# An attention and quantised-linear kernel: regrouped opening tiles, a reordered DMA queue in seven units, and q loads issued by ScalarE

## The chip, the cores and the metric

The kernel runs on one core of a Trainium2 chip. The metric is the device time of one execution in microseconds (us). Three runs of the kernel before gave 1568.5, 1568.98 and 1569.91 us, so the median is 1568.98.

## What is computed

```python
x  = L0_attn_x                              # 8 x 1024 x 256, f32
xn = layernorm(x)
q  = xn @ Wq.T   # 16 heads of 16;   k, v = xn @ Wk.T, xn @ Wv.T   # 8 kv heads, each used by 2 heads
energy = q @ k.T - |i - j| * 2 ** -(head + 1)
attn   = softmax(energy / 4) @ v
ffn    = int8(round(xn / x_scale)) @ weight_q.T * x_scale * weight_scale + bias   # x_scale = max|xn| / 127 per token
out    = x + (attn @ Wo.T + bo) + ffn
```

## The kernel before, in words

There are 64 tiles of 128 tokens (`TILES`) and 64 **units**, one for each pair of batch element and kv head (`UNITS`, `KV_HEADS` = 8, two query heads each). Every engine runs a program of its own, written out by hand; semaphores join them.

**Tiles.** A tile is normalised, turned, multiplied by the weights of q and k, and q and k are split into three bf16 parts. The parts are stored to `parts_dram`; tokens' scales go by `token_dram`. The first 11 tiles (`PREP_AHEAD`) are made before any unit, in one loop on each of PE, ScalarE (`find_high`, `keep_xn_t`, `find_middle`), VectorE (`normalise`, `first_stats`, `find_first_largest`, `find_rest`) and GpSimd (`find_rstd`, `find_low`). Tiles 2 and 3 of each four use the buffer `parts_more`: `wait_stored` holds tile 7 until tile 3 is stored. Later tiles are made two at a time in odd units, at block c = 1.

**Sets.** A unit needs a set: rows of k and of q for two heads, copied by DMA from `parts_dram` into one of four slots (`k_set`, `q_set`). `load_set` issues 11 loads (5 of k, 3 of q for each head) and, from set 3 on, two more with the rows of the position bias. Sets 0 to 2 are loaded at the start: set 0 needs tiles 0 to 7. `load_again` copies part of a set to other partitions, after waiting for the whole set. `place_max(u)` puts the negated row maxima of unit u into the set, in four small DMAs. `store_att` and `load_att_t` carry the attention output. All of these DMAs are issued by SP, in program order: a wait in one of them holds every later one.

**Units.** In unit u PE computes, in 8 blocks (c), four score halves (`col_half`), the row scores of later units (`ahead_row_block`: head 1 of unit u+1 in blocks 0 to 3, head 0 of unit u+2 in blocks 4 to 7), and `pv_block`. ScalarE exponentiates each half, GpSimd multiplies the diagonal block (`weigh_near`), VectorE reduces the row scores (`reduce_block`, 16 per unit). PE can begin unit u only when its set is whole, with the four DMAs of `place_max(u)`. `place_max(u + 1)` waits for `turn_max(u + 1)`, which VectorE runs in block 5 of unit u.

**Late sets.** Sets 8, 16, ..., 56 (`late_set`) need tiles that are only just stored. They are loaded at the very end of the unit three before, and unit u = 6, 14, ..., 54 has to run `load_again(u + 2)` early, on a load that is still in flight. SP's order in such a unit is: next x, x turned, `load_again(u + 2)`, set u+3, the token load, `place_max(u + 1)`, `store_att(u - 1)`, `load_att_t`, `load_again(u + 3)`.

**Opening rows.** Before unit 0, PE runs 24 row blocks (`first_row_block`: units 0 and 1), each read by one reduction, with other work between them (`first_others`, placed by `OTHERS_BEHIND` behind blocks 1, 2, 4, 6, ...): `make_v(t)` waits until ScalarE has kept the previous v (`keep_v`).

Of the kernel before, what the change touches and what calls it, by code (L numbers as in the profile page):

```python
# [35 lines left out]
P = 128  # L36
# [153 lines left out]
def build(nc, x, x_t, wqk_t, wv_t, wo_t, wo_last_t, w8_t, w_scale, bias_attn, bias_lin, q_alibi, k_alibi, diag,  # L190
          eye, parts_dram, token_dram, att_dram, out):
    ctx = ExitStack()
    with ctx:
# [232 lines left out]

        block = ctx.enter_context(nc.Block())
# [3 lines left out]
        def _(sp):  # L431
# [20 lines left out]
            def load_set(u, slot):  # L452

                g, tok = u % KV_HEADS, (u // KV_HEADS) * SEQ

                def rows(dst, chunk, row, pick, loaded=set_loaded[slot]):
                    for at, q_parts, k_parts in PAIRS:
                        use = q_parts if pick == "q" else k_parts
                        n = len(use)
                        cols = bass.ds(chunk * TOKENS + tok, SEQ)  # L460
                        here = dst[at:at + n * HEAD_DIM, :]
                        if len(set(use)) == 1:
                            src = parts_dram[bass.ds(row, HEAD_DIM), use[0]:use[0] + 1, cols]
                            sp.dma_start(here, src.rearrange("d j n -> j d n").broadcast_to(  # L464
                                [n, HEAD_DIM, SEQ])).then_inc(loaded, 16)
                        elif list(use) == sorted(use):
                            src = parts_dram[bass.ds(row, HEAD_DIM), use[0]:use[0] + n, cols]
                            sp.dma_start(here, src.rearrange("d j n -> j d n")).then_inc(loaded, 16)  # L468
                        else:
                            for j, part in enumerate(use):  # L470
                                src = parts_dram[bass.ds(row, HEAD_DIM), part:part + 1, cols]
                                sp.dma_start(here[j * HEAD_DIM:(j + 1) * HEAD_DIM, :],  # L472
                                             src.rearrange("d j n -> (d j) n")).then_inc(loaded, 16)

                pairs = KV_HEADS // (QK_CHUNKS - 1)
                rows(k_set[:, slot, :], QK_CHUNKS - 1, g * HEAD_DIM, "k",
                     first_rows_loaded if u == 0 else set_loaded[slot])
                for e in range(GROUP):
                    rows(q_set[:, slot, e, :], g // pairs, (g % pairs * GROUP + e) * HEAD_DIM, "q",
                         first_rows_loaded if u == 0 and e == 0 else set_loaded[slot])  # L480
                if u >= SETS - 1:
                    load_alibi(u, slot)
# [118 lines left out]
            def unit(u, f):  # L601
# [18 lines left out]
                if f["token"]:  # L620
                    load_token(u + 1 + PREP_AHEAD)
                if not f["last"]:
                    place_max(u + 1, (u + 1) % SETS)
                if f["prev"] and u % PAIR == 0:
                    store_att(u - 1)
                for t in f["next_att"]:
                    load_att_t(t, t % 2)
# [39 lines left out]
        def _(pool):  # L667
# [182 lines left out]
            def unit(u, f):  # L850
                t = u + PREP_AHEAD
                for c in range(BLOCKS):
# [12 lines left out]
                    if c == 3:  # L865
                        for made in f["made"][1:]:
                            split_middle(made)
                    if c == 4:
# [621 lines left out]
```

## Time and profile before

| | |
|---|---|
| median of three runs | 1568.98 us |
| the profiled execution, whole time | 1568.38 us |
| its span in the trace | 1566.4 us |
| PE busy | 1497.0 us, 96% |
| VectorE busy | 1394.6 us, 89% |
| ScalarE busy | 1184.8 us, 76% |
| GpSimd busy | 1076.1 us, 69% |
| chain that ended last | PE 47%, VectorE 30%, SP's queue 9%, issue 8%, DMA 3% |

Time is counted from the start of the span. A unit's start, wherever it is given, is the start of the first exponential of that unit on ScalarE. PE is TensorE, DVE VectorE, ACT ScalarE, POOL GpSimd, SP the engine that issues DMAs; SPq is time in which it issues one. PEclk is the granted clock of TensorE, 1.00 being full speed. "L464" is line 464 of the kernel.

### The profile page before, as it was taken

The page shows a single profiled execution, that of the slowest core. Times are in us where ns is not written, and L with a number is a line of the kernel's source. Part 1 is how long each engine was busy: PE and PEld are TensorE (multiplying, and loading weights), DVE is VectorE, ACT ScalarE, POOL GpSimd, SP SyncE. Part 2 cuts the span into 40 slices and gives each one's busy share as a digit, 9 for nine tenths or more (in the row PEclk, how much of TensorE's full clock was granted, in tenths as well). Part 3 has the DMA queues.
Part 4 walks back from the last instruction along what each step waited for, and adds up shares of the span by engine and source line. Part 5 has one row for each costly group of instructions (what it writes and reads, how often), then busy time and mean ns, then how long its engine had stood idle before and what let it go on. Part 6 is the DMA issues. An engine that isn't in the chain of part 4 may idle for free.

```text
span 1566.4 us, 42517 instructions
## 1 busy us (share of the span) xinstructions
PE 1497.0 (96%) x16284; PEld 583.0 (37%) x16284; DVE 1394.6 (89%) x1698; ACT 1184.8 (76%) x2331; POOL 1076.1 (69%) x1627
## 2 busy tenths in 40 slices
PE   5899999999999999999989999999999999999998
PEld 5333333333333333333333334333333333333333
DVE  5999989999899998999979999899998988999981
ACT  3467777777787776887767887777877777788885
POOL 5467777777788876787757877677877776533332
PEclk9999999999999999999999999999999999999999
DMA  6522243333334334333333433433333332312212
GB/s 169 140 76 71 74 100 81 93 98 81 105 83 108 96 79 109 91 92 101 84 92 94 105 85 91 103 98 96 97 83 96 94 92 65 82 49 68 72 44 62
DMA packets 197291, 140.98 MB, mean 90 GB/s; under 512 B 107040, under 2 KB 165728, under 8 KB 197088
## 3 DMA queue, kind: packets, MB, share of 16 engines
q1 hardware_dynamic: 197088, 138.27, 34.2%
q8 instruction: 129, 2.11, 0.6%
q14 instruction: 74, 0.61, 0.1%
HBM read 81.40 MB, written 35.63 MB: 75 GB/s over the span
## 4 chain that ended last, share of the span: by engine, by line
PE 47%; DVE 30%; SPq 9%; issue 8%; DMA 3%; POOL 2%; ACT 0%; POOLq 0%; DVEq 0%; ACTq 0%
DVE row_max L999 27%; PE ps_ring L1279 15%; PE ps_pv L1355 13%; PE ps_row L1296 9%; PE ps_ring L1395 4%; PE ps_ring L1415 3%; SPq L464 2%; SPq L468 2%; SPq L506 2%; DMA q<-neg_max_t 1%; SPq L472 1%; PE ps_ring L1398 1%; DMA k<-k_alibi 1%; DVE pv_turned L1039 1%; PE ps_ring L1409 1%
## 5 line engine op out<-in xcount | busy, mean ns | idle before, releaser
L999 DVE TENSOR_REDUCE row_max<-ps_row 128x1 f32<-128x1024 f32 x1024 | 1199.5, 1213 | 114.7 <-PE ps_row L1298 99.4
L1171 ACT ACTIVATE probs<-ps_ring 128x512 f32<-128x512 f32 x2048 | 1084.5, 601 | 245.2 <-PE ps_ring L1279 242.6
L1279 PE MATMUL ps_ring<-q,k 122*32 122x512 bf16 x8192 | 636.6, 383 | 19.9 <-DMA q<-neg_max_t 19.0
L762 POOL TENSOR_TENSOR probs<-probs,near 128x256 f32<-128x256 f32 x512 | 375.2, 733 | 324.8 <-ACT probs L1171 318.9
L1355 PE MATMUL ps_pv<-probs,v_unit 128*32 128x512 f32 x4096 | 533.5, 596 | 0.0
L1279 PEld LDWEIGHTS ps_ring<-q,k 122*32 122x32 bf16 x8192 | 215.1, 95 | 518.0 <-ACT probs L1171 324.7
L1296 PE MATMUL ps_row<-k,q 64*128 64x512 bf16 x944 | 326.2, 385 | 25.8 <-DVE row_max L999 11.4
L1298 PE MATMUL ps_row<-k_again,q_again 64*128 64x512 bf16 x944 | 326.0, 385 | 0.0
L1296 PEld LDWEIGHTS ps_row<-k,q 64*128 64x128 bf16 x944 | 84.2, 93 | 320.3 <-issue 199.6
L1355 PEld LDWEIGHTS ps_pv<-probs,v_unit 128*32 128x32 f32 x4096 | 124.7, 110 | 54.2 <-issue 7.7
L1298 PEld LDWEIGHTS ps_row<-k_again,q_again 64*128 64x128 bf16 x944 | 84.0, 92 | 0.0
L817 POOL CAST parts<-qk 128x384 bf16<-128x384 f32 x53 | 26.7, 504 | 83.2 <-ACT qk L1180 83.2
L1395 PE MATMUL ps_ring<-xn_t,wqk 128*128 128x128 f32 x636 | 79.9, 275 | 0.5 <-ACT probs L1171 0.5
L1395 PEld LDWEIGHTS ps_ring<-xn_t,wqk 128*128 128x128 f32 x636 | 77.0, 192 | 2.5 <-ACT probs L1171 1.3
L1039 DVE STREAM_TRANSPOSE pv_turned<-ps_pv 128x512 f32<-128x512 f32 x64 | 45.2, 707 | 28.4 <-PE ps_pv L1355 28.4
L809 POOL TENSOR_SCALAR xq_t<-xround 128x256 bf16<-128x256 f32 x53 | 57.4, 1082 | 4.5
L801 POOL TENSOR_SCALAR xround<-xt_step 128x256 f32<-128x256 f32 x53 | 57.0, 1076 | 4.5
L689 POOL TENSOR_TENSOR parts<-rest,parts 128x384 bf16<-128x384 f32 x59 | 54.2, 918 | 8.0 <-ACT parts L1127 3.7
L1177 ACT ACTIVATE v_all<-ps_ring 128x128 f32<-128x128 f32 x53 | 14.7, 278 | 58.5 <-PE ps_ring L1398 58.5
L1415 PE MATMUL ps_ring<-wo,att_t 128*128 128x256 f32 x224 | 57.3, 382 | 0.0
L1279 PE MATMUL ps_row<-k,q 120*32 120x512 bf16 x640 | 45.3, 390 | 11.9 <-issue 9.1
L819 POOL TENSOR_TENSOR rest<-qk,parts 128x384 f32<-128x384 f32 x53 | 48.6, 918 | 4.3
(84 smaller groups left out, 1012.0 us busy)
## 6 DMA issues: line engine op xcount, KB each, us to landing
parts_dram<-parts SPq DMA_DIRECT2D x59, 288.0 KB, 3.0
q_again<-q SPq DMA_DIRECT2D x63, 256.0 KB, 3.3
token_b<-token_dram SPq DMA_DIRECT2D x53, 256.0 KB, 4.1
q<-parts_dram SPq DMA_DIRECT2D x128, 96.0 KB
k<-parts_dram SPq DMA_DIRECT2D x256, 32.0 KB
q<-parts_dram SPq DMA_DIRECT2D x128, 64.0 KB
att_dram<-att_unit SPq DMA_DIRECT2D x126, 64.0 KB
att_t<-att_dram SPq DMA_DIRECT2D x56, 128.0 KB, 2.9
```

The lines of the kernel that those rows point to most:

```text
L762: pool.tensor_tensor(here, here, near[:, u % KV_HEADS, :].rearrange("p (e n) -> p e n", e=GROUP), ALU.mult).then_inc(weighted, 1)
L801: pool.tensor_scalar(xround[:, :], xt_step[:, 1, :, :].rearrange("p c n -> p (c n)"), Q_MAX, ROUND, ALU.min, ALU.add).then_inc(xt_rounded, 1)
L809: pool.tensor_scalar(xq_t[:, t % TURNED, :, :].rearrange("p c n -> p (c n)"), xround[:, :], -ROUND, -Q_MAX - 1, ALU.add, ALU.max).then_inc ...
L999: dve.tensor_reduce(row_max[:, par, e, qb:qb + 1], ps_row[qb % 2][:, :], AX_X, ALU.max, negate=True).then_inc(row_max_found, 1)
L1039: dve.transpose(pv_turned[:, :], ps_pv[:, :]).then_inc(pv_read, 1)
L1171: act.activation(probs[:, c % PBUFS, e, h * HALF:(h + 1) * HALF], ring_bank(u, c, e, h), ACT.Exp, scale=SCALE).then_inc(ring_freed, 1)
L1279: mm = pe.matmul(to[at, :], weights[:, at], moving, start=start, stop=stop)
L1296: pe.matmul(ps_row[qb % 2][:, 0:HALF], q_set[0:ROW_K, slot, e, at], k_set[0:ROW_K, slot, 0:HALF], start=True, stop=True)
L1298: pe.matmul(ps_row[qb % 2][:, HALF:SEQ], q_again[ROW_K:2 * ROW_K, u % AGAIN, e, at], k_again[ROW_K:2 * ROW_K, u % AGAIN, :], start=True, s ...
L1355: mm = pe.matmul(ps_pv[32 * j:32 * j + 32, :], v_unit[:, par, c, :], probs[:, c % PBUFS, j // 2, (j % 2) * HALF:(j % 2 + 1) * HALF], start ...
L1395: pe.matmul(bank[:, m * P:(m + 1) * P], wqk[:, c, m * P:(m + 1) * P], xn_t[:, t % TURNED, c, :], start=(c == 0), stop=(c == EC - 1))
L1415: mm = pe.matmul(bank[:, EMBED:2 * EMBED], att_t[:, t % 2, c, :], wo[:, c, :], start=(c == 0), stop=(c == EC - 1))
```

## The change

Six edits:
1. **Opening tiles regrouped.** Tiles 0 to 7 are made first, on every engine. The maxima of those tiles, the statistics of 8 and 9, the scales, and then tiles 8, 9 and 10 follow behind them. Before, all 11 ran in one loop with the maxima inside.
2. **q of sets 0 to 2 by ScalarE.** ScalarE issues these 18 loads behind `find_middle` of tile 10. SP issues the 15 loads of k where it issued both.
3. **SP's order in units 6, 14, ..., 54** (`copied`): token load, `load_again(u + 2)`, `place_max(u + 1)`, `store_att(u - 1)`, `load_att_t`, and only then set u+3. At the end `load_again(u + 3)` as before.
4. **Attention output in even units:** `norm` on GpSimd moves from the end of block 3 into block 4; on VectorE the reciprocal goes from behind row block 5 to behind 7 and `turn_back` from behind 13 to behind 11.
5. **VectorE's tile work in units 0 and 1** is split between block 1 and block 3.
6. **Projections of the last two units** (`project_last`) are issued two at a time (`project_pairs`), and four instead of six come behind the last block.

```diff
@@ load_set on SP
+                load_rows(sp, k_set[:, slot, :], QK_CHUNKS - 1, tok, g * HEAD_DIM, "k", ...)
+                if u >= SETS - 1:
+                    load_q(sp, u, slot)
                 if u >= SETS - 1:
                     load_alibi(u, slot)
@@ unit on SP
-                if u + 2 < UNITS and late_set(u + 2):
+                copied = u + 2 < UNITS and late_set(u + 2)
+                if copied:
+                    if f["token"]:
+                        load_token(u + 1 + PREP_AHEAD)
                     load_again(u + 2, (u + 2) % SETS)
+                    place_max(u + 1, (u + 1) % SETS)
+                    store_att(u - 1)
+                    for t in f["next_att"]:
+                        load_att_t(t, t % 2)
                 if f["row_set"] and not late_set(u + 3):
                     next_set(u + 3)
...
-                if f["token"]:
-                    load_token(u + 1 + PREP_AHEAD)
...
+                if not copied:
+                    if f["token"]:
+                        load_token(u + 1 + PREP_AHEAD)
...
@@ the opening on GpSimd
-            for t in range(PREP_AHEAD):
-                if t + 4 < PREP_AHEAD:
+            for t in range(BLOCKS):
+                if t + 4 < BLOCKS:
                     find_rstd(t + 4, t % 2)
+                find_low(t, t % 2)
+            for t in range(BLOCKS, PREP_AHEAD):
+                find_rstd(t, t % 2)
+            for t in range(BLOCKS, PREP_AHEAD):
                 find_low(t, t % 2)
@@ the opening on VectorE
-            for t in range(PREP_AHEAD):
-                if t + 2 < PREP_AHEAD:
+            for t in range(BLOCKS):
+                if t + 2 < BLOCKS:
                     normalise(t + 2, t % 2)
-                if t + 4 < PREP_AHEAD:
+                if t + 4 < BLOCKS:
                     first_stats(t + 4)
-                if t + 2 < PREP_AHEAD:
-                    find_first_largest(t + 2)
                 find_rest(t, t % 2, early[t % 2][1])
+            for t in range(BLOCKS, BLOCKS + 2):
+                first_stats(t)
+            for t in range(BLOCKS):
+                find_first_largest(t)
+            find_first_scales(0, BLOCKS, 0)
+            for t in range(BLOCKS, BLOCKS + 2):
+                normalise(t, t % 2)
+            first_stats(PREP_AHEAD - 1)
+            find_rest(BLOCKS, 0, early[0][1])
+            normalise(PREP_AHEAD - 1, 0)
+            for t in range(BLOCKS + 1, PREP_AHEAD):
+                find_rest(t, t % 2, early[t % 2][1])
@@ the opening on ScalarE
+            for t in range(BLOCKS, BLOCKS + 2):
+                keep_xn_t(t, early[t % 2][0])
+            for t in range(BLOCKS, PREP_AHEAD):
                 find_high(t, early[t % 2][1])
                 if t + 2 < PREP_AHEAD:
                     keep_xn_t(t + 2, early[t % 2][0])
                 find_middle(t, t % 2)
+            for i in range(FIRST_PARTS):
+                act.wait_ge(first_parts_stored[i], 16 * len(range(i, BLOCKS, FIRST_PARTS)))
+            for u in range(SETS - 1):
+                load_q(act, u, u)
@@ the opening on PE
+            for t in range(BLOCKS, BLOCKS + 2):
+                turn_xn(t, early[t % 2][0])
+            for t in range(BLOCKS, PREP_AHEAD):
                 make_qk(t, early[t % 2][1])
@@ unit on VectorE
-                at_sums, at_norm = (5, BLOCKS) if apart else (3, 3)
+                at_sums, at_norm = (BLOCKS - 1, SLOTS) if apart else (3, 3)
+                made = 1 if u < PAIR else PAIR
...
-                        if i == SLOTS - 3 and apart:
+                        if i == BLOCKS + 3 and apart:
                             turn_back(u - 1)
-                    if c == 1:
-                        for t in f["normed"]:
+                    if c in (1, 3):
+                        for t in f["normed"][here(c)]:
...
@@ the last units on PE
+            def project_pairs(u, c):
+                at = (u - UNITS + 2) * BLOCKS + c - BLOCKS // 2
+                if 0 <= at < BLOCKS and at % 2 == 0:
+                    for i in (at, at + 1):
+                        project_last(0, P, i)
+                if u == UNITS - 1 and c in (BLOCKS - 3, BLOCKS - 1):
+                    for i in (c - BLOCKS + 3, c - BLOCKS + 4):
+                        project_last(1, P - GROUP * HEAD_DIM, i)
```

## Rows read from the trace of the kernel before

**Rows 1.** Waits over the span: who waited for what, us, times, longest.
```profile
PE ps_ring L1279 <- DMA q<-neg_max_t: 19.0, 8, 4.3
```
**Rows 2.** Busy time in stretches, each two whole units: 12-13, 6-7, 14-15, 30-31, 54-55.
```profile
350.49:396.73 46.24, 45.57 (x494) 17.69 (x492) 43.30 (x53) 36.52 (x73) 37.50 (x57) 1.00 0.31 78
208.53:258.00 49.47, 46.30 (x534) 17.17 (x532) 43.19 (x53) 36.09 (x72) 36.28 (x55) 0.97 0.38 96
396.73:446.61 49.88, 46.35 (x542) 18.53 (x540) 43.40 (x53) 36.85 (x74) 37.56 (x57) 1.00 0.40 104
...
775.60:828.17 52.57, 47.81 (x542) 18.71 (x540) 43.40 (x53) 36.93 (x73) 35.56 (x54) 0.97 0.39 102
...
1342.89:1386.84 43.95, 42.43 (x506) 14.54 (x504) 40.34 (x41) 34.93 (x68) 18.33 (x30) 1.00 0.31 82
```
**Rows 3.** Timeline of SP, 396 to 448 us: start, duration, line, transfer, count.
```profile
400.19 0.83 SPq L488 DMA_DIRECT2D k<-k_alibi  x2
...
405.15 0.55 SPq L497 DMA_DIRECT2D k_again<-k  x1
...
424.18 0.71 SPq L468 DMA_DIRECT2D k<-parts_dram  x1
...
430.56 0.83 SPq L488 DMA_DIRECT2D k<-k_alibi  x2
...
434.35 5.61 SPq L440 DMA_DIRECT2D parts_dram<-parts  x2
...
440.77 2.80 SPq L506 DMA_DIRECT2D q<-neg_max_t  x4
```
**Rows 4.** Transfers over the span: KB each, median us from issue to landing.
```profile
token_dram<-token SPq DMA_DIRECT2D x53, 2.0 KB, 4.5
```
**Rows 5.** Timelines of VectorE and of GpSimd, unit 14.
```profile
409.62 0.20 DVE L1017 STREAM_TRANSPOSE neg_max_t<-neg_max 128x32 bf16<-128x32 bf16 x1
...
408.29 0.62 POOL L752 TENSOR_TENSOR att_normed<-pv_turned,rsum 128x256 f32<-128x256 f32 x1
```
**Rows 6.** Timeline of SP, 0 to 80 us.
```profile
29.77 0.72 SPq L468 DMA_DIRECT2D k<-parts_dram  x1
...
32.36 1.10 SPq L464 DMA_DIRECT2D q<-parts_dram  x2
33.51 0.73 SPq L468 DMA_DIRECT2D q<-parts_dram  x1
```
**Rows 7.** Timeline of ScalarE, 0 to 80 us; in brackets the idle time before, and its releaser.
```profile
24.34 0.49 ACT L1121 ACTIVATE probs<-ps_row 128x384 bf16<-128x384 f32 x1 [1.01 <-DMA parts_dram<-probs]
...
30.25 0.52 ACT L1127 ACTIVATE probs<-rest 128x384 bf16<-128x384 f32 x1 [0.62 <-DVE rest L963]
```
**Rows 8.** Timeline of VectorE, 0 to 80 us.
```profile
18.41 0.39 DVE L931 TENSOR_REDUCE amax_first<-probs 128x1 f32<-128x256 f32 x1
...
24.86 0.56 DVE L963 TENSOR_TENSOR rest<-ps_row,probs 128x384 f32<-128x384 f32 x1 [0.75 <-ACT probs L1121]
...
43.97 12.77 DVE L999 TENSOR_REDUCE row_max<-ps_row 128x1 f32<-128x1024 f32 x11 [0.69 <-PE ps_row L1279]
...
60.21 9.17 DVE L999 TENSOR_REDUCE row_max<-ps_row 128x1 f32<-128x1024 f32 x8
```
**Rows 9.** Timeline of PE, 0 to 122 us.
```profile
10.87 2.34 PE L1230 MATMUL ps_row<-probs,wqk 128*128 128x128 f32 x12
...
16.63 1.50 PE L1230 MATMUL ps_row<-probs,wqk 128*128 128x128 f32 x12
...
37.98 1.90 PE L1279 MATMUL ps_row<-k,q 120*32 120x512 bf16 x16 [9.06 <-issue]
...
68.72 0.61 PE L1279 MATMUL ps_ring<-q,k 122*32 122x512 bf16 x8 [0.60 <-DMA q<-neg_max_t]
...
102.89 0.39 PE L1296 MATMUL ps_row<-k,q 64*128 64x512 bf16 x1 [1.91 <-DVE row_max L999]
```
**Rows 10.** Busy time and granted clock in one stretch of the opening.
```profile
33.00:43.00 10.00, 5.02 (x33) 2.60 (x34) 4.75 (x9) 0.28 (x1) 4.34 (x7) 0.51 0.48 120
```

More of the change, by code:

```diff
@@ L425, in wait_stored, with load_rows, load_q @@
                 eng.wait_ge(parts_stored[t % 2], 16 * ((t - PREP_AHEAD) // 2))
+        def load_rows(eng, dst, chunk, tok, row, pick, loaded):
+            for at, q_parts, k_parts in PAIRS:
+                use = q_parts if pick == "q" else k_parts
+                n = len(use)
+                cols = bass.ds(chunk * TOKENS + tok, SEQ)
+                here = dst[at:at + n * HEAD_DIM, :]
+                if len(set(use)) == 1:
+                    src = parts_dram[bass.ds(row, HEAD_DIM), use[0]:use[0] + 1, cols]
+                    eng.dma_start(here, src.rearrange("d j n -> j d n").broadcast_to(
+                        [n, HEAD_DIM, SEQ])).then_inc(loaded, 16)
+                elif list(use) == sorted(use):
+                    src = parts_dram[bass.ds(row, HEAD_DIM), use[0]:use[0] + n, cols]
+                    eng.dma_start(here, src.rearrange("d j n -> j d n")).then_inc(loaded, 16)
+                else:
+                    for j, part in enumerate(use):
+                        src = parts_dram[bass.ds(row, HEAD_DIM), part:part + 1, cols]
+                        eng.dma_start(here[j * HEAD_DIM:(j + 1) * HEAD_DIM, :],
+                                      src.rearrange("d j n -> (d j) n")).then_inc(loaded, 16)
+        def load_q(eng, u, slot):
+            g, tok, pairs = u % KV_HEADS, (u // KV_HEADS) * SEQ, KV_HEADS // (QK_CHUNKS - 1)
+            for e in range(GROUP):
+                load_rows(eng, q_set[:, slot, e, :], g // pairs, tok, (g % pairs * GROUP + e) * HEAD_DIM, "q",
+                          first_rows_loaded if u == 0 and e == 0 else set_loaded[slot])
         block = ctx.enter_context(nc.Block())
@@ L454, in load_set @@
                 g, tok = u % KV_HEADS, (u // KV_HEADS) * SEQ
[L456 to L480, printed above, removed]
+                load_rows(sp, k_set[:, slot, :], QK_CHUNKS - 1, tok, g * HEAD_DIM, "k",
+                          first_rows_loaded if u == 0 else set_loaded[slot])
+                if u >= SETS - 1:
+                    load_q(sp, u, slot)
                 if u >= SETS - 1:
@@ L619, in unit @@
                     load_att_last(1, P - GROUP * HEAD_DIM, UNITS - 1)
-                if f["token"]:
-                    load_token(u + 1 + PREP_AHEAD)
[L622 to L627, printed above, removed]
+                if not copied:
+                    if f["token"]:
+                        load_token(u + 1 + PREP_AHEAD)
+                    if not f["last"]:
+                        place_max(u + 1, (u + 1) % SETS)
+                    if f["prev"] and u % PAIR == 0:
+                        store_att(u - 1)
+                    for t in f["next_att"]:
+                        load_att_t(t, t % 2)
                 if f["row_set"]:
@@ L867, in unit @@
                             split_middle(made)
+                    if c == 4 and f["prev"] and u % PAIR == 0:
+                        norm(u - 1)
                     if c == 4:
@@ L892, in unit @@
                                 add_weighted(made)
-                    if c == 3 and f["prev"] and u % PAIR == 0:
-                        norm(u - 1)
                     if c == 1:
@@ L1090, in unit @@
                             find_scale(t, t % 2)
-                        for t in f["stats"]:
+                        for t in f["stats"][here(c)]:
                             wait(dve, x_loaded, 16 * (t - X_AHEAD + 1))
@@ L1237, in _ @@
             pe.wait_ge(wqk_loaded, 16)
-            for t in range(PREP_AHEAD):
+            for t in range(BLOCKS):
+                make_qk(t, early[t % 2][1])
+                if t + 2 < BLOCKS:
+                    turn_xn(t + 2, early[t % 2][0])
+            for t in range(BLOCKS, BLOCKS + 2):
+                turn_xn(t, early[t % 2][0])
+            for t in range(BLOCKS, PREP_AHEAD):
                 make_qk(t, early[t % 2][1])
```

22 lines of the change are left out of this document (10 added, 12 removed).

## The prediction

> **What bounds the kernel now.** I read the opening first, since the change rewrites it, then the units. In the opening ([rows 6 to 9]) PE makes tiles at about 1.65 us each until tile 7, which is held: ScalarE's copy of it starts at 24.34 us, when tile 3's store has landed [rows 7]. SP starts to load set 0 at 29.77 us [rows 6], PE starts the first row block at 37.98 us [rows 9], and from there VectorE sets the pace: 24 reductions, the last eight from 60.21 us on, end at 69.4 us [rows 8]. Unit 0 starts then; PE waits 0.6 us for the maxima's DMA [rows 9].
>
> In the units PE is the bound: a usual pair of units takes 46.24 us with PE busy for 45.57 of it [rows 2]. The exceptions are the seven pairs that begin with units 6, 14, ..., 54. There PE waits for the row maxima's DMA, 19.0 us in eight waits [rows 1]. The pairs take 49.47, 49.88, ..., 43.95 us, 345.9 us for the seven together [rows 2]. The reader is to see why in SP's timeline: it idles from about 402.4 us to 405.15 for set 16's landing, then issues set 17 and only later the maxima of unit 15, though VectorE had them turned at 409.82 us [rows 3, 5].
>
> **Part 1, tiles 0 to 7.** The maxima taken out of the loop (0.39 us each [rows 8]) free VectorE, but not the path: tile 7 still waits for tile 3's store, whose issue hangs on GpSimd's `find_rstd` and `find_low` of tiles 0 to 3, and these are unchanged. I cost it at nothing: SP still starts set 0 at 29.8 us.
>
> **Part 2, tiles 8 to 10, and q behind them.** Now ScalarE starts q of set 0 only behind tile 10. Before, its last opening copy ended at 30.77 us [rows 7], and SP did not wait for it. Counting on from the difference of tile 7 (24.86 + 0.56 = 25.4 us [rows 8]): two statistics 1.1, eight maxima 2.5 (they start about every 0.3 us), scales 0.6, so tile 8 is normalised at 29.8 us. From there it is a chain of turn, copy, product, copy, difference and copy, with tile 10's turn behind tile 8's difference. With PE at full speed (12 products in 1.50 us) it ends at 39.0 us; with PE at half speed (2.34 us) [rows 9] at 42.2 us. PE has idled for 7 us by then, and the trace has the clock at 0.51 in the stretch after PE's idle time there [rows 10]. I take 40.8 us.
> - Three q loads cost SP 1.10 + 0.73 us [rows 6], 1.87 with the gap. ScalarE's own price is not in the trace; I take SP's. So q of set 0, head 0 is issued at 42.7 us.
> - From the end of that issue to PE's start it took 37.98 - 34.24 = 3.7 us [rows 6, 9]. So the first row block comes at 46.4 us, **8.4 us later** than 37.98. Bounds: 39.0 + 1.9 + 2.7 = 43.6 and 42.2 + 1.9 + 4.1 = 48.2 us, 5.6 to 10.2 us later.
> - ScalarE goes on issuing: six groups of 1.87 are 11.2 us, to 52.0 us. Behind that in its queue are `keep_v(0)` and everything else that PE's `first_others` need. PE's `make_v(1)`, behind row block 2, waits for it; row block 3 and all later ones are queued behind `make_v(1)`. The fourth reduction comes at about 52.0 + 0.3 + 1.0 + 0.4 + 0.8 = 54.5 us; without the wait it would be 46.4 + (43.97 - 37.98) = 52.4 us [rows 8, 9]. **2.1 us more**; bounds 0 (cheap issues) and 4.
> - SP saves the 18 issues (11 us), but this is worth only the 0.6 us that PE waited for the maxima's DMA [rows 9]: **-0.6 us**. Behind that wait VectorE's reductions are the next bound.
>
> The Trainium skill, DMA: Bandwidth & Descriptors, section Issuing engines are not separate DMA queues, says that DMAs issued from several engines run on the same 16 DMA engines and save only the issuer's time. That speaks against a gain from the second queue beyond these issues; the sum takes none.
>
> **Part 3, VectorE's tile work in units 0 and 1.** In unit 1 PE waits 1.91 us for a reduction that stands behind two tiles' work [rows 9]. Half of that work moves two blocks on. I take 1.5 us off in unit 1 and 0.6 in unit 0, **-2.1 us**; bounds 0 and -3.9 us, the latter if the half-speed stretch of the clock behind this wait goes too.
>
> **Part 4, SP's order in the seven units.** In unit 14, which starts at 396.73 us, `load_again(16)` still goes at 405.15 and ends at 406.3 us [rows 3]. The maxima of unit 15 go at 409.85 us, five and a half earlier, 2.7 us for four. They land in time, and unit 14 ends at 417.6 us (its usual 20.26 us and 0.6 for the dearer row blocks of set 16) instead of 420.41. That is the gain. Now what is pushed behind it, item by item:
> - `store_att`, `load_att_t` to 415.0; set 17, 7.2 us as set 18 took, from 424.18 to 431.39 [rows 3], to 422.3.
> - `load_again(17)` before followed six microseconds of other issues; now it stands directly behind its own set. The landing took 405.15 - 401.02 = 4.1 us [rows 3]: 426.4, issued at 427.6. This is a **new wait**.
> - the store of out, x, x turned: 429.2. Set 18: 436.5. `store_att`: 437.75. Tokens: stored from 437.8 to 439.4 us. Parts, both ready by then: 440.9 us.
> - the token load waits for the token store, 4.5 us [rows 4]: 442.3 us. The maxima of unit 16 go at 442.75 us, and the fourth at 444.85. PE starts 3.1 us after the fourth issue, as at the end of unit 14 before. Unit 16 starts at **447.9 us; before it was 446.61**.
>
> So SP, not PE, ends unit 15: it would have taken 26 us and takes 30. Before, unit 15 had 4 us of SP's idle time inside (the wait for the second tile's parts, inside the 5.61 us of [rows 3]); the change uses that up and more. The same count for the others gives: pair 6-7 +0.1, 14-15 +1.3, 22-23 -0.3, 30-31 -1.4, 38-39 +2.1, 46-47 +1.8, 54-55 +1.3 us, where the maxima of unit 56 stand behind two whole sets. Together **+4.9 us**.
>
> The pairs before that are long beyond this, as 30-31 with 52.57 us, had the clock at half speed for 3.4 us behind PE's wait: PEclk 0.97 over the pair, and PE busy 47.81 instead of 46.35 us [rows 2]. So one such drop costs 1.4 us, and three of the seven pairs had one. The waits of 3 to 4 us are still there, one unit later. I count two drops: **+2.8 us**. Bounds for the whole of part 4: -3 us (set 17 lands faster, no drops) and +13.
>
> **Part 5, the rest.** `norm` on GpSimd (0.62 us [rows 5]) comes behind block 4's product, at 411.1 us by unit 14's clock. VectorE's `turn_back` now stands behind row block 11, at 412.3: 1.2 us of cover, so nothing. If the cover went, each late microsecond would stop PE's row blocks in 31 even units. The paired projections move 0.7 us from the end into the last unit; I cost them at nothing, between -0.5 and +0.9 us.
>
> **The sum.** 8.4 + 2.1 - 0.6 - 2.1 + 4.9 + 2.8 = 15.5 us on the profiled execution's 1568.4, which is 0.6 us under the median, less than the runs differ. **Forecast 1584 us.**
>
> **Rivals.**
> - *The reorder pays in full (the other side).* If SP catches up in units 7, 15, ..., every pair goes to its usual length and a little: 46.1 + 5 x 47.1 + 43.1 = 324.7 us, 21 us less than before. With the opening at +7.8 us the time is 1568.4 + 7.8 - 21.2 = **1555 us**. It decides at the maxima of unit 16: they would have to be issued 4 us earlier than by my count, at 438.7 instead of 442.75 us. For it: SP's 4.2 idle microseconds before. Against it: the 4.1 us landing has nothing to hide it.
> - *ScalarE issues a DMA at almost no cost.* Then head 0's rows come 1.7 us earlier and the 2.1 us stall is gone: **1580 us**. The Trainium skill, DMA: Bandwidth & Descriptors, section Anatomy of one DMA, puts a sequencer's dispatch at about 50 ns, for the GpSimd path; 18 issues would be 0.9 us by it. SP's rows of 0.4 to 0.7 us per DMA do not agree.
> - *Nothing to see.* The opening's chain at full clock, a quick landing, no stall, and the pairs even: 5.6 - 0.6 - 3.9 + 1 = 2 us, **1570 us**. For it: every term is at its low bound, and that is also what speaks against it.
> - *The cover of `turn_back` is gone.* Half a microsecond in each of 31 even units: 1584 + 15 = **1599 us**. Against it: the margin of 1.2 us counted above, which is the same in every even unit.
>
> **How the numbers follow.** Forecast 0.64, cheap issues 0.10, nothing 0.08, full gain 0.08, cover gone 0.05, the rest spread. The forecast's own range is 1575 to 1594 us. For 8 in 10 the range takes in the cheap issues and most of "nothing": 1569 to 1595 us. A measurement of this kernel tells about 0.2% (3 us) from no change. Faster by more than that: 0.10 (the full gain and a little of the low ends); within: 0.08; slower: 0.82.
>
> **What the profile would show.** Right: the first row block at 44 to 48 us; a PE gap of about 2 us behind the third row block; ScalarE's queue issuing for 11 us before its first `keep_v`; units 6, 14, ... with 20.9 us, units 15, 23, ... with about 30 us, and PE waiting for `q<-neg_max_t` there; SP idle 4 us before the `load_again` behind set 17. Wrong: a first row block before 43 us, which would mean that tile 7 or tiles 8 to 10 come earlier than counted; or units 15, 23, ... of 26 us.

## The result and the profile after

The changed kernel takes 1609.74 us (median of four runs, 1608.14 to 1612.09), the kernel before 1568.74 on the same chip: a ratio of **1.0269**, 95% interval 1.0242 to 1.0296. The forecast was 1584 us with a range up to 1595. The direction is right, the size is not. The profiled execution took 1608.14 us, with a span of 1606.0, 39.6 more than before.

The page of the changed kernel (busy time, and the chain that ended last), and then its waits: who waited for what, us, times, longest.

```profile
span 1606.0 us, 42519 instructions
PE 1507.6 (94%) x16284; PEld 585.5 (36%) x16284; DVE 1399.4 (87%) x1698; ACT 1186.6 (74%) x2331; POOL 1076.8 (67%) x1627
PE 38%; DVE 37%; SPq 8%; issue 8%; DMA 5%; POOL 2%; ACTq 1%; ACT 0%; POOLq 0%; DVEq 0%
...
PE ps_ring L1328 <- DMA q<-neg_max_t: 34.9, 7, 7.2
...
ACT v_all L1189 <- issue: 15.6, 1, 15.6
```

PE's wait for the row maxima's DMA did not go: 34.9 us in seven waits, where it was 19.0 in eight [rows 1]. And PE is *busier* by 10.6 us for the same 16284 matmuls, which is the clock. Busy time of whole units (us, PE, PEld, VectorE, ScalarE, GpSimd, PEclk, DMA share, GB/s): the pairs 6-7, 14-15 and 30-31 of the changed kernel, and its unit 16; the last line is unit 16 of the kernel before.

```profile
220.28:270.08 49.80, 44.74 (x532) 17.04 (x530) 43.33 (x53) 35.97 (x72) 38.77 (x58) 1.00 0.35 91
410.72:463.43 52.71, 46.42 (x540) 18.54 (x538) 43.54 (x53) 36.72 (x73) 40.66 (x61) 0.98 0.37 96
797.48:850.13 52.65, 46.41 (x540) 18.50 (x538) 43.54 (x53) 36.70 (x74) 38.73 (x58) 0.98 0.36 97
463.43:486.47 23.04, 22.64 (x230) 6.54 (x226) 19.75 (x20) 17.10 (x32) 14.88 (x23) 0.89 0.29 76
```

```profile
446.61:466.87 20.26, 19.86 (x226) 6.30 (x224) 19.43 (x20) 16.89 (x34) 18.44 (x29) 1.00 0.27 76
```

Pair 14-15 took 49.88 us before and takes 52.71 [rows 2]. Unit 16, whose DMA order the change leaves alone, goes from 20.26 to 23.04 us, at a granted clock of 0.89. Edit 4 does touch it, but e2 below has edit 4 and keeps the 20.26 us. From the starts of all units the 39.6 us divide like this:

| where | before | after | difference | forecast |
|---|---|---|---|---|
| start of the first row block | 37.98 | 45.80 | +7.8 | +8.4 |
| from there to the fourth reduction | 5.99 | 11.03 | +5.0 | +2.1 |
| from there to unit 0 | 25.28 | 25.24 | 0.0 | -0.6 |
| units 0 and 1 | 48.66 | 48.12 | -0.5 | -2.1 |
| seven pairs 6-7, ..., 54-55 | 345.9 | 358.4 | +12.5 | +4.9 |
| units 8, 16, ..., 56, behind them | 141.8 | 155.4 | +13.6 | +2.8 |
| units 62 and 63 | 41.43 | 42.87 | +1.4 | 0 |
| all other units | | | -0.2 | 0 |

**SP in unit 15.** Timeline of SP in the changed kernel: start, duration, line, transfer, count. Unit 15 starts at 431.45 us.

```profile
436.01 0.83 SPq L494 DMA_DIRECT2D k<-k_alibi  x2
441.06 0.55 SPq L503 DMA_DIRECT2D k_again<-k  x1
...
451.05 0.82 SPq L494 DMA_DIRECT2D k<-k_alibi  x2
451.92 1.18 SPq L522 DMA_DIRECT2D att_dram<-att_unit  x2
453.14 0.95 SPq L566 DMA_DIRECT2D token_dram<-token  x2
454.14 2.22 SPq L467 DMA_DIRECT2D parts_dram<-parts  x2
458.38 0.33 SPq L574 DMA_DIRECT2D token_b<-token_dram  x1
458.74 2.80 SPq L512 DMA_DIRECT2D q<-neg_max_t  x4
```

The new wait is there: set 17 is issued by 436.84 us, and its copy goes at 441.06, 4.2 us later. SP then never idles, except for the token's way through DRAM: the store is issued at 453.14 us, the load at 458.38. The maxima of unit 16 go 27.3 us into unit 15; VectorE had them ready at 18.5. What this does to PE (its timeline, idle time and releaser in brackets, and two stretches with the granted clock):

```profile
462.70 1.04 PE L1328 MATMUL ps_ring<-q,k 122*32 122x512 bf16 x8 [5.81 <-DMA q<-neg_max_t]
```

```profile
463.43:470.00 6.57, 6.57 (x48) 1.47 (x48) 3.52 (x4) 3.85 (x7) 1.80 (x3) 0.60 0.57 137
470.00:476.00 6.00, 5.76 (x72) 1.89 (x64) 6.00 (x7) 4.36 (x9) 4.77 (x7) 1.00 0.37 114
```

PE waits 5.81 us, and the eight matmuls behind the wait take 1.04 us where they took 0.61 [rows 9]: the lower of the two levels, 1.2 GHz. The clock is back at full speed before 470 us. Six of the seven pairs are followed by such a stretch. The units behind them, 8, 16, ..., 48, are 1.90, 2.78, 1.53, 2.34, 2.05 and 2.78 us longer than before, behind waits for the maxima's DMA of 4.2, 5.8, 5.1, 5.8, 7.2 and 5.1 us. Unit 56 is 0.22 us longer at full clock, behind a wait of 1.7 us; so about 0.2 us of each is something else than the clock.

**The opening.** Timelines of ScalarE, VectorE and PE in the changed kernel:

```profile
37.90 0.52 ACT L1158 ACTIVATE probs<-rest 128x384 bf16<-128x384 f32 x1 [0.62 <-DVE rest L981]
38.04 1.58 ACTq L436 DMA_DIRECT2D q<-parts_dram  x2
39.65 0.74 ACTq L440 DMA_DIRECT2D q<-parts_dram  x1
...
49.76 3.16 ACTq L436 DMA_DIRECT2D q<-parts_dram  x2
52.95 0.71 ACTq L440 DMA_DIRECT2D q<-parts_dram  x1
54.04 0.28 ACT L1189 ACTIVATE v_all<-ps_ring 128x128 f32<-128x128 f32 x1 [15.61 <-issue]
```

```profile
56.83 2.36 DVE L1025 TENSOR_REDUCE row_max<-ps_row 128x1 f32<-128x1024 f32 x2 [5.72 <-PE ps_row L1328]
```

```profile
45.80 1.90 PE L1328 MATMUL ps_row<-k,q 120*32 120x512 bf16 x16 [9.24 <-issue]
...
54.37 1.22 PE L1295 MATMUL ps_ring<-wv,probs 128*128 128x128 f32 x4 [4.54 <-ACT v_all L1189]
```

Tile 10 ends on ScalarE at 38.42 us, 7.6 later than before [rows 7]. Then ScalarE issues for 15.6 us; `make_v(1)` on PE waits 4.54 us for its first copy behind that, and VectorE stands idle for 5.72 us before the fourth reduction.

### The profile page after: what moved, and what is told of

It reads as the page before. It is cut to its first block, busy times and chain, and to the rows that moved or that the text cites. A ratio compares the mean times of both kernels' runs of the same rounds, so it can differ in the third digit from the quotient of the medians.

```text
span 1606.0 us, 42519 instructions
## 1 busy us (share of the span) xinstructions
PE 1507.6 (94%) x16284; PEld 585.5 (36%) x16284; DVE 1399.4 (87%) x1698; ACT 1186.6 (74%) x2331; POOL 1076.8 (67%) x1627
## 4 chain that ended last, share of the span: by engine, by line
PE 38%; DVE 37%; SPq 8%; issue 8%; DMA 5%; POOL 2%; ACTq 1%; ACT 0%; POOLq 0%; DVEq 0%
DVE row_max L1025 33%; PE ps_ring L1328 11%; PE ps_pv L1404 10%; PE ps_row L1345 7%; PE ps_ring L1449 3%; PE ps_ring L1469 3%; SPq L436 2%; DMA token_dram<-token 2%; SPq L440 2%; DMA k<-k_alibi 2%; DVE pv_turned L1065 1%; SPq L444 1%; PE ps_row L1328 1%; PE ps_ring L1452 1%; SPq L512 1%
## 5 line engine op out<-in xcount | busy, mean ns | idle before, releaser
L1328 PE MATMUL ps_ring<-q,k 122*32 122x512 bf16 x8192 | 640.5, 385 | 37.1 <-DMA q<-neg_max_t 34.9
```

The lines of the kernel that those rows point to most:

```text
L1328: mm = pe.matmul(to[at, :], weights[:, at], moving, start=start, stop=stop)
```

## The experiments

Twelve kernels, each timed beside the kernel before (median 1570 to 1572 us there). The diffs are excerpts (`...` stands for lines not shown). They show e1, e6, e7, e9 and e10 against the kernel before, e2, e8 and e11 against the changed kernel, e3 against e1, e4 and e5 against e3, and e12 against e5.

**e1_order_only.** Edits 3 and 4 alone.

```diff
+                copied = u + 2 < UNITS and late_set(u + 2)
+                if copied:
+                    if f["token"]:
+                        load_token(u + 1 + PREP_AHEAD)
                     load_again(u + 2, (u + 2) % SETS)
+                    place_max(u + 1, (u + 1) % SETS)
...
```

> Edits 3 and 4 alone on the kernel before (SP's order in units 6, 14, ..., 54; norm and turn_back moved). Theory A (SP is late in units 7, 15, ..., PE idles there for 5 to 7 us, and the clock falls behind each of these waits): the seven pairs cost 12 to 13 us and units 8, 16, ..., 56 another 13 us, as in the changed kernel; 1594 us, ratio 1.017. Rival B (the half-speed stretches come from the changed opening or its shift in time, and the order costs only its 5 us, as I had forecast): 1574 us, ratio 1.003, units 8, 16, ... at 20.3 us.

1591.49 us, ratio 1.0128 (1.0099 to 1.0157). Pair 14-15 and unit 16 in its profile:

```profile
397.41:450.44 53.03, 46.42 (x540) 18.52 (x538) 43.53 (x53) 36.69 (x74) 40.67 (x61) 0.98 0.36 95
450.44:473.11 22.67, 22.28 (x230) 6.50 (x226) 19.75 (x20) 17.11 (x33) 14.88 (x23) 0.90 0.29 77
```

The seven pairs take 358.4 us, as in the whole change, and the units behind them 156.0 (155.4). So both the longer pairs and the clock belong to SP's order (edit 4, which is in here too, is cleared by e2) and not to anything that the opening leaves behind. Theory A holds, with a median 2.5 us under its number.

**e2_all_but_order.** All edits but edit 3.

```diff
-                copied = u + 2 < UNITS and late_set(u + 2)
-                if copied:
-                    if f["token"]:
-                        load_token(u + 1 + PREP_AHEAD)
+                if u + 2 < UNITS and late_set(u + 2):
                     load_again(u + 2, (u + 2) % SETS)
-                    place_max(u + 1, (u + 1) % SETS)
...
```

> The changed kernel with edit 3 undone: SP has the order of before in units 6, 14, ..., 54. Theory A: only the opening (+12.8 us), units 0 to 5 (-1) and the last two units (+1.4) are left: 1582 us, ratio 1.008. Rival B: 1600 us or more, with half-speed stretches in the units.

1583.6 us, ratio 1.0083 (1.0058 to 1.0108), as A said. Unit 0 starts at 84.43 us, the seven pairs take 346.3 us and the units behind them 141.8, as before. The two halves together make 1.021; the whole change is at 1.0269, and the intervals overlap. The spans of the profiled executions add up better: 25.3 us more in e1 and 16.7 in e2, 42.0 together, where the whole change has 39.6.

**e3_again_behind_k.** e1, with the landing of set 8k+1 given cover: `load_again(8k+1)` goes in unit 8k-1, between the k and the q loads of the next set, and not directly behind its own set.

```diff
@@ unit 8k-1 on SP
-                    next_set(u + 3)
+                    next_set(u + 3, "k")
+                    load_again(u + 2, (u + 2) % SETS)
+                    next_set(u + 3, "q")
@@ end of unit 8k-2
-                    else:
+                    elif not copied:
                         load_again(u + 3, (u + 3) % SETS)
```

> Edits 3 and 4, and one thing more: load_again(8k+1) is not waited for at the end of unit 8k-2 but issued in unit 8k-1 behind the five k loads of the next set, when its set has landed. Theory A: SP's wait of about 4.5 us is gone, the maxima of unit 16 go at about 23 us into unit 15 instead of 27.3, the pair takes about 48.2 us instead of 52.7, and the clock falls seldom: 1564 us, ratio 0.997. Rival C (SP is late by the number of its issues; the wait is filled with other waits, as the token's): 1585 us or more, ratio 1.01.

1555.14 us, ratio 0.990 (0.9873 to 0.9927): better than either theory. Pair 14-15 and unit 16:

```profile
392.38:440.62 48.24, 46.20 (x540) 18.48 (x538) 43.52 (x53) 36.69 (x73) 39.04 (x59) 1.00 0.41 105
440.62:461.10 20.48, 20.09 (x230) 6.30 (x226) 19.74 (x20) 16.94 (x33) 16.53 (x26) 1.00 0.31 85
```

Giving cover to one wait of 4.2 us, in seven places, was worth 36 us by the medians. In the profiles the pairs fall from 358.4 to 328.6 us, and the units behind them from 156.0 to 143.1: PE's waits in the pairs are now 1.8 us or less, and no stretch at half clock follows one of them. (These two profiles differ by more, 42.7 us: e1's is of its slowest run, e3's of its fastest.)

**e4_untangled.** e3, and the stores of the attention output and of the tokens go between the k and the q loads, so that the token's landing is covered too.

```diff
                     load_again(u + 2, (u + 2) % SETS)
+                    store_att(u - 1)
+                    for t in f["normed"]:
+                        store_token(t)
                     next_set(u + 3, "q")
```

> As e3_again_behind_k, and in units 7, 15, ..., 55 the attention output and the tokens are stored between the k loads and the q loads of the next set, so that the token load finds them landed. Theory A: the maxima of unit 16 go at about 21 us into unit 15, early enough for its usual length of 26 us; pairs of about 47 us, no wait for the maxima, no half-speed stretch after unit 2: 1548 us, ratio 0.987. Rival C: no better than e3_again_behind_k by more than 3 us.

1557.47 us, ratio 0.9918 (0.9893 to 0.9944): no better than e3, as the rival said. Its SP, in unit 15:

```profile
437.72 1.56 SPq L440 DMA_DIRECT2D parts_dram<-parts  x2
439.38 1.92 SPq L571 DMA_DIRECT2D token_b<-token_dram  x1
```

The token load no longer waits for the store, but issuing it takes 1.92 us behind the stores of the parts (0.33 us in the changed kernel), and the maxima go again 23 us into the unit. So the token's way through DRAM was hardly what made the load late: from the end of the parts' stores to the end of this load it is 2.0 us here and 2.4 in the changed kernel.

**e5_place_first.** e3, and in units 8k-1 the maxima's DMAs go ahead of the parts and the token load.

```diff
                     for t in f["normed"]:
                         store_token(t)
+                    place_max(u + 1, (u + 1) % SETS)
...
-                    if not f["last"]:
+                    if not f["last"] and not late_set(u + 1):
                         place_max(u + 1, (u + 1) % SETS)
```

> As e3_again_behind_k, and in units 7, 15, ..., 55 the maxima's DMAs go before the stores of the parts and the token load. Theory A: they go at about 19 us into the unit, so the unit keeps its usual 26 us and the seven pairs give back another 5 to 6 us: 1548 us, ratio 0.986. Rival D (PE or VectorE ends those units by now, or the token that is loaded later holds GpSimd in the next unit): within 2 us of e3_again_behind_k.

1545.64 us, ratio **0.9844** (0.9812 to 0.9876), as expected. SP in unit 15, which starts at 413.85 us, and the pair's row:

```profile
430.22 0.95 SPq L563 DMA_DIRECT2D token_dram<-token  x2
432.58 2.73 SPq L509 DMA_DIRECT2D q<-neg_max_t  x4
435.36 1.36 SPq L440 DMA_DIRECT2D parts_dram<-parts  x2
```

```profile
393.14:439.85 46.71, 46.23 (x542) 18.67 (x540) 43.54 (x53) 36.60 (x74) 37.42 (x57) 1.00 0.38 103
```

The maxima go 18.7 us into the unit, as soon as VectorE has them. The seven pairs take 322.9 us, PE busy for nearly all of it, and inside the units PE has no wait above 1 us for that DMA. The prediction's first rival put full payment at 324.7 us and its condition at maxima 4 us earlier than forecast: this kernel, not the changed one, meets it.

**e6_regroup_alone.** Edit 1 alone; SP still issues all loads.

```diff
-            for t in range(PREP_AHEAD):
+            for t in range(BLOCKS):
                 make_qk(t, early[t % 2][1])
...
+            for t in range(BLOCKS, BLOCKS + 2):
+                turn_xn(t, early[t % 2][0])
```

> Edit 1 alone on the kernel before: the opening's tiles regrouped, SP issues q and k of all sets. Theory A (the cost of the opening is that q waits in ScalarE's queue behind tile 10, and that ScalarE's own work waits behind the 18 issues): SP loads set 0 at 27.8 us, tiles 8 to 10 end at 38.4 us while it lands, the first row block comes at about 38.3 us and unit 0 starts at 69.5 us; 1569 us, ratio 1.000. Rival E (the regrouping itself delays the row blocks by the later tiles 8 to 10): the first row block at 43 us or later, 1575 us.

1575.49 us, ratio 1.0035 (1.0011 to 1.006). Rival E is right, though its first row block was to come at 43 us or later and comes at 42.52: the regrouping costs by itself. PE and VectorE in its opening:

```profile
42.52 1.05 PE L1304 MATMUL ps_row<-k,q 120*32 120x512 bf16 x16 [3.54 <-DVE w L1005]
```

```profile
50.34 12.86 DVE L1011 TENSOR_REDUCE row_max<-ps_row 128x1 f32<-128x1024 f32 x11 [1.12 <-PE ps_row L1304]
```

PE's first row block doesn't wait for q here but for VectorE's cast of the weights (`w8`, line 1005), which stands behind the last tile. The prediction had not seen this second way from tile 10 to the row blocks. The fourth reduction is at 50.34 us (43.97 before [rows 8]), and unit 0 starts 5.6 us later. Of that, 4.5 us are the later first row block; the first reduction also has to wait until VectorE has done its other opening work, at 45.65 us.

**e7_act_q_alone.** Edit 2 alone: the tiles as before, the 18 q loads by ScalarE.

```diff
                 find_middle(t, t % 2)
+            for i in range(FIRST_PARTS):
+                act.wait_ge(first_parts_stored[i], 16 * len(range(i, BLOCKS, FIRST_PARTS)))
+            for u in range(SETS - 1):
+                load_q(act, u, u)
```

> Edit 2 alone on the kernel before: ScalarE issues q of sets 0 to 2 behind tile 10, which ends at 30.8 us there. Theory A: the issues last 15.6 us, to 46.4 us; the first row block comes at about 38.5 us, but row block 3 waits for ScalarE and comes at about 49 us instead of 43.3; unit 0 starts 5.6 us later; 1575 us, ratio 1.004. Rival F (the stall of 5.7 us belongs to PE's low clock in the regrouped opening): no gap, unit 0 at about 69 us, 1569 us.

1570.72 us, ratio 1.0004 (0.9987 to 1.002). VectorE, ScalarE and SP in its opening:

```profile
40.67 1.23 DVE L1005 TENSOR_REDUCE row_max<-ps_row 128x1 f32<-128x1024 f32 x1 [0.63 <-PE ps_row L1290]
45.21 2.36 DVE L1005 TENSOR_REDUCE row_max<-ps_row 128x1 f32<-128x1024 f32 x2 [3.31 <-PE ps_row L1290]
```

```profile
42.42 0.28 ACT L1157 ACTIVATE v_all<-ps_ring 128x128 f32<-128x128 f32 x1 [12.60 <-DMA parts_dram<-parts]
```

```profile
32.97 6.57 SPq L467 DMA_DIRECT2D parts_dram<-probs  x1
39.58 6.59 SPq L589 DMA_DIRECT2D near_bias<-diag  x1
46.21 4.34 SPq L440 DMA_DIRECT2D k<-parts_dram  x1
```

A's mechanism is there, a gap of 3.31 us before the fourth reduction; but the first row block also comes 1.4 us earlier (36.59 us), so the fourth reduction is only 1.2 us later than before and unit 0 starts at 70.77 us (69.25 before), too little for the time to show. F's number is the one that holds, though its cause does not. Edit 2's cost depends on where its issues start: 29.44 us here, 38.04 in the whole change, and they last 12.6 us here, 15.6 there. 8.6 + 3.0 = 11.6 us, which is the distance of the two fourth reductions (45.21 and 56.83).

Single DMAs of SP take 4.3 to 6.6 us to issue here; the first two begin while ScalarE issues, the third when it has ended. ScalarE's queue is not needed for a slow issue: in the kernel before, where SP issues alone, the same store of parts takes 4.06 us. The Trainium skill, DMA: Bandwidth & Descriptors, section Issuing engines are not separate DMA queues, says that several issuing engines share the same 16 DMA engines. These rows time the issuing alone, and no run here shows whether that sharing slows it.

**e8_act_q_of_set_0.** Edits 1 and 2, but ScalarE issues only q of set 0, six loads.

```diff
-            for u in range(SETS - 1):
-                load_q(act, u, u)
+            load_q(act, 0, 0)
...
-                if u >= SETS - 1:
+                if u > 0:
                     load_q(sp, u, slot)
```

> Edits 1 and 2, but ScalarE issues only the six q loads of set 0; SP issues those of sets 1 and 2. Theory A: the first row block still comes at 45.8 us, since q of set 0 still waits behind tile 10, but the gap of 5.7 us before the fourth reduction is gone; unit 0 starts at about 77 us, 7.8 us later than before; 1577 us, ratio 1.005. Rival F: the gap stays.

1576.6 us, ratio 1.0037 (1.002 to 1.0054), as A said. The first row block is as late as in the whole change (46.64 us), and VectorE's gap is gone:

```profile
47.73 2.36 DVE L1017 TENSOR_REDUCE row_max<-ps_row 128x1 f32<-128x1024 f32 x2 [3.50 <-PE ps_row L1314]
50.72 14.07 DVE L1017 TENSOR_REDUCE row_max<-ps_row 128x1 f32<-128x1024 f32 x12 [0.63 <-PE ps_row L1314]
```

So the gap of 5.72 us is the price of the other 12 loads in ScalarE's queue.

**e9_pairs_alone.** Edit 6 alone.

```diff
                     ahead_row_block(u, f, 2 * c + 1)
+                    project_pairs(u, c)
...
-            project_last(1, P - GROUP * HEAD_DIM, 2)
             pv_block(UNITS - 1, (UNITS - 1) % 2, BLOCKS - 1)
```

> Edit 6 alone: the last units' projections in pairs. Theory A (the 1.4 us by which units 62 and 63 are longer after the change belong to this edit: their work now stands inside unit 63 and waits there for the attention output's load): units 62 and 63 take 42.8 us where they took 41.4, all else as before, time 1570, ratio 1.001. Rival T (the 1.4 us come from what the changed order of the attention output leaves behind, not from the pairs): units 62 and 63 as before, time 1568.5, ratio 1.000; a look at the two units decides, the time can't.

1572.9 us, ratio 1.0013 (0.9989 to 1.0037): not to be told from no change. The units decide: 42.87 us for 62 and 63, exactly the length in the whole change, so A holds. PE at the end of unit 63, in this kernel:

```profile
1556.49 1.03 PE L1355 MATMUL ps_pv<-probs,v_unit 128*32 128x512 f32 x8
1558.17 1.06 PE L1355 MATMUL ps_pv<-probs,v_unit 128*32 128x512 f32 x8 [0.64 <-POOL probs L762]
```

and in the kernel before:

```profile
1555.38 0.70 PE L1387 MATMUL ps_row<-wo,att_last 96*128 96x256 f32 x2
1556.09 1.06 PE L1355 MATMUL ps_pv<-probs,v_unit 128*32 128x512 f32 x8
```

The projection that stood before the last product used the time in which PE otherwise waits for GpSimd. Moved into the unit, it takes PE's time there, and the wait of 0.64 us stays empty. That is not yet half of the 1.4 us; where the rest goes is not shown. The theory's other half, a wait for the attention output's load, is not it: PE has no idle time above 0.3 us behind that load.

**e10_split_alone.** Edit 5 alone.

```diff
-                    if c == 1:
-                        for t in f["normed"]:
+                    if c in (1, 3):
+                        for t in f["normed"][here(c)]:
```

> Edit 5 alone: VectorE's tile work of units 0 and 1 split between two blocks. Theory A (as forecast: PE's wait for a reduction in unit 1 halves, and the stretch at half clock behind it goes): units 0 and 1 take 46.5 us where they took 48.66, time 1566.5, ratio 0.999. Rival S (the half that moves two blocks on holds a reduction there, and the clock drops as before): 48.1 us or more, as in the changed kernel, and no change of the time.

1569.01 us, ratio 0.998 (0.996 to 1.0): a small gain at the edge of what can be told. Units 0 and 1 take 46.04 us, as A said. Unit 1 of the kernel before, unit 0 of the changed kernel and unit 0 of this one:

```profile
91.49:117.91 26.42, 23.70 (x244) 8.11 (x242) 23.58 (x33) 17.85 (x37) 16.39 (x25) 0.94 0.29 75
```

```profile
82.07:105.67 23.60, 20.39 (x214) 5.83 (x210) 21.81 (x26) 16.94 (x34) 12.38 (x20) 0.93 0.23 64
```

```profile
68.61:90.39 21.78, 18.95 (x214) 5.75 (x210) 21.11 (x26) 16.94 (x33) 12.61 (x21) 1.00 0.34 90
```

Before, the clock fell in unit 1 (0.94, 1.6 us of PE's time). In the whole change unit 1 is free of it, but unit 0 has a stretch of its own (0.93, 1.4 us more than here). Alone, the edit has neither. But this is one profile, and where the clock falls in these two units changes from profile to profile without the edit too: e1, with the opening and the tile work of before, has the stretch in unit 0 and none in unit 1. At full clock, unit 0 takes 22.24 us before and 21.79 here, unit 1 25.0 in e1 and 24.25 here. So about 1.2 of the 2.6 us are surely the edit's, and the rest may be luck with the clock.

**e11_all_place_first.** The whole change with the order of e5.

```diff
+                    next_set(u + 3, "k")
+                    load_again(u + 2, (u + 2) % SETS)
+                    next_set(u + 3, "q")
...
+                    place_max(u + 1, (u + 1) % SETS)
```

> The whole change, but with the order of e5_place_first in the eight places: what is left is the price of the opening and of the last units. Theory A (the parts add up, and the half-speed stretches behind long PE waits come from SP's order alone): 1545.6 of e5 + 12.8 of the opening + 1.4 of the last units - 0.5 of units 0 and 1 = 1559 us, ratio 0.994; units 15, 23, ... take 26 us and units 16, 24, ... 20.3. Rival G (the opening disturbs the later rhythm too, so that it costs more than its own 12.8 us): 1564 us or more.

1561.71 us, ratio 0.9923 (0.9894 to 0.9951). A holds, 2.7 us above its sum and under G's bound: units 15, 23, ... take 26.0 us, the units behind the pairs 20.26, and the seven pairs (seven places, not the eight of the expectation) 322.4 us. Three DMA groups in another order take the whole change from 2.7% slower than before to 0.8% faster. Against e5 the opening, at 85.46 us here, and the last two units (42.88) are what is left.

**e12_place_first_q0.** e5, the tiles as before, ScalarE issuing q of set 0 alone.

```diff
+            load_q(act, 0, 0)
...
+                if u > 0:
+                    load_q(sp, u, slot)
```

> e5_place_first, with the opening's tiles as before, and ScalarE issuing q of set 0 alone (6 loads) while SP issues the rest: the part of edit 2 that should pay. Theory A (q of set 0 on a second queue lets PE start 1.4 us earlier, and six issues are too few to hold the values' copies behind them): unit 0 starts 1 to 1.5 us earlier, 1544.4 us, ratio 0.9835. Rival H (VectorE's 24 reductions begin earlier, but SP's issues are slowed while ScalarE issues, so that later sets and the maxima come as late as before): 1545.6 us or more, unit 0 at 69.2 us or later.

1544.79 us, ratio 0.9816 (0.9789 to 0.9843), the fastest median of all, but its runs (1543.07 to 1546.5) overlap with those of e5 (1544.41 to 1548.33). Unit 0 starts at 69.52 us; in the seven profiles with the opening of before, edit 5 or not, it starts between 68.23 and 70.97. Neither A nor H is settled: the effect is smaller than this scatter.

## Why the prediction was wrong, point by point

The step that failed is in part 4: the clock behind PE's waits, counted as two drops of 1.4 us. The seven waits for the maxima came out longer than counted, six of them were followed by a stretch at half clock, and the units behind the pairs grew by 13.6 us instead of 2.8. The measured span is 24.1 us above the sum of the forecast (39.6 for 15.5). The clock is 10.8 of that, the pairs 7.6, ScalarE's queue 2.9, the two first units 1.6 and the paired projections 1.4. The rest cancels. With the measured cost of the clock in place of the counted one the forecast would have been 1595 us, the end of its range, and the kernel took 1609.74: the clock is the largest error and not the only one.

**Part 1 and tile 7.** SP starts set 0 at 27.79 us (29.77 before [rows 6]), though the prediction left that unchanged. About half of this is scatter: in the five profiles with the regrouped tiles it starts between 27.79 and 28.94 us, in the nine others between 28.82 and 30.28. Tiles 8 and 9 are normalised by 28.18 us, where 29.8 was counted for tile 8 alone, and that is most of why the tiles ended at 38.42 us and not at 40.8.

**Part 2, the first row block.** +8.4 forecast, +7.8 measured, but by errors that cancel: that the number is so near is luck. The tiles' chain ended 2.4 us earlier than counted, within its bounds. But the three loads took 2.35 us to issue (38.04 to 40.39), not 1.87, and PE started 5.4 us behind them, not 3.7. And e6 shows a second condition, VectorE's cast of the weights. In the whole change that cast was done by 39.97 us and held nothing, but without the q loads it would have kept the first row block from coming before that time.

**Part 2, ScalarE's queue.** The mechanism is right, the term mis-sized: 18 issues took 15.6 us, not 11.2, since some pairs took 2.55 and 3.16 us, and the fourth reduction was held 5.0 us, not 2.1, above the bound of 4. The 0.6 us of PE's wait for the maxima gave nothing: from the fourth reduction to unit 0 it is 25.24 us where it was 25.28, VectorE's pace.

**Part 3.** -2.1 forecast, -0.5 measured. Alone the edit gives -2.6 (e10), part of it by luck with the clock. In the whole change a stretch at half clock in unit 0 takes most of it back; the forecast had none there.

**Part 4, the pairs.** The step by step count of SP's queue is right in kind: unit 14 ends 20.73 us after its start (20.86 forecast), the wait behind set 17 is 4.2 us (4.1), SP ends unit 15. Its items are too small, each by a little: counted from unit 15's start, the second copy ends at 10.8 us (10.0 forecast), set 18 at 20.4 (18.9), the parts at 24.9 (23.3), the token load goes at 26.9 (24.7), and the first of the maxima at 27.3 (25.2). The parts' stores took 2.22 us for 1.5, set 18 0.3 us more, and the token load went 5.2 us behind its store where the landing was put at the 4.5 of [rows 4]. The forecast took that landing for the reason why the load goes late; by e4 nearly as much time passes behind the parts without it. In pair 38-39, the worst one (54.07 us for 49.12), the wait behind the set was 5.1 us. Seven pairs: +12.5 us and not +4.9.

**Part 4, the clock.** This is the step that failed, and the largest part of the miss: two drops at 1.4 us were counted because three of the seven pairs before had one. The waits before were 2.4 us on average and 4.3 at most [rows 1]; the prediction put the new ones at "3 to 4 us", and six of the seven are 4.2 to 7.2. All six were followed by a stretch at half clock that reached into the next unit, +13.6 us with the 0.2 us of each that is not the clock. The price of a drop was taken from a row where it was small, and its frequency was not raised with the length of the wait.

The fourteen profiles (twelve experiments, before and after) have 65 waits of PE above 1 us behind unit 1, all for the maxima's DMA. Of 14 waits of 4.2 us or more all were followed by half clock, of 39 waits of 2.1 to 3.7 us 19 were, and of 12 waits of 1.1 to 2.0 us none was. This is a count and no rule: in unit 1, where PE waits for VectorE, a wait of 1.91 us was followed by half clock in the kernel before and not in e5. What decides in the range between is open.

**Part 5.** The cover of `turn_back` held; usual even units still take 20.26 us. The paired projections cost 1.4 us, above the bound of 0.9 (e9).

**The rivals.** Full payment of the reorder had its condition stated rightly (the maxima of unit 16 about 21 us into unit 15): this order has them at 27.3, e5 at 18.7. Cheap issues on ScalarE are refuted by 15.6 us for 18 DMAs. What was missing is a rival on the far side: every landing in the chain a little longer, and the clock lost after every wait.

What stays open is why some issues take 2 to 6 us: the runs show it mostly when two queues issue or behind the stores of the parts, not which resource is short. The same opening starts unit 0 anywhere from 68.2 to 71.0 us, and a part of that is such issues: in the three late profiles (e4, e5, e9) the four DMAs of the first maxima take 3.6 to 4.4 us to issue and PE waits 1.7 to 2.2 us for them, in the others 2.8 to 3.1 us and 0.8 us or less.

## What to carry to other kernels

When a DMA queue is reordered, write down its whole order to the *next* point where compute needs it: a wait moved to where nothing covers it (a copy directly behind its own load) makes late whatever stands last in the queue. Put the small transfers that compute waits for ahead of the bulk ones as soon as their data is ready; here these two moves turned 2.7% slower into 0.8% faster. And price a long wait of PE with the half-speed stretch behind it: here that came to as much again (13.6 us) as the longer pairs (12.5 us).

## What the runs showed of the hardware

- Issuing a DMA has no fixed price. Two q loads took 1.06 to 1.12 us on SP in most places, up to 1.88 in some, and 1.09 to 3.16 on ScalarE; one DMA of SP took up to 6.59 us that began while ScalarE issued (e7) and 4.06 with SP alone (before), and the token load 0.33 us or 1.92, by what stood before it (e4).
- A landing has no fixed time either. The load behind a token's store, 2 KB, went 5.2 us after the store's issue (such a store landed after 4.5 us before, the median of [rows 4]); set 17's copy could go 4.2 us after the last load of the set, that of pair 38-39 5.1 us after it.
- Behind PE waits of 4.2 to 7.2 us the granted clock was at its lower level (1.2 GHz) in six of six cases of the changed kernel, and the next unit was 1.5 to 2.8 us longer; the longest wait did not have the dearest stretch (2.05 us behind 7.2, 2.78 behind 5.1 and 5.8). Over all profiles it was 14 of 14 waits from 4.2 us up, and 19 of 39 from 2.1 to 3.7.
